# A graph network kernel on one Trainium2 core: two rings of one-hot sets, and the weighted copies dealt anew between GpSimd and ScalarE

## What is computed

```
agg = jax.ops.segment_sum(x[src], tgt, num_segments=n)              # layers 0, 3: plain counts
out = jax.ops.segment_sum(support[src] * edge_weight[:, None], dst)  # layer 1: weighted
agg = jax.ops.segment_sum(concat(nodes[src], edges) @ W_message, dst) # layer 2
```

## Time and profile before

| | |
|---|---|
| median of 3 runs | 1917.61 us (1917.14 to 1918.48) |
| the profiled execution's own time | 1919.31 us |
| its span (first to last instruction) | 1917.4 us |
| PE busy | 1701.7 us (89%), 11659 matmuls |
| DVE busy | 1092.2 us (57%) |
| ACT busy | 759.1 us (40%) |
| POOL busy | 369.2 us (19%) |
| mean granted TensorE clock | 0.952 of 2.4 GHz |
| build stage, first to last L1271 | 46.0 to 577.8 us |

### The profile page before, as it was taken

One profiled execution on the slowest core, in us unless ns is written; L12 is line 12 of the kernel. 1 busy time (PEld: TensorE's weight loads), 2 busy tenths in 40 slices (PEclk: granted clock), 3 DMA queues, 4 the chain that ended last, 5 costly groups with the idle time before them and its releaser, 6 DMA issues.

```text
span 1917.4 us, 47392 instructions
## 1 busy us (share of the span) xinstructions
PE 1701.7 (89%) x11659; PEld 1292.2 (67%) x11660; DVE 1092.2 (57%) x3183; ACT 759.1 (40%) x2194; POOL 369.2 (19%) x982
## 2 busy tenths in 40 slices
PE   2999899999990999999997999999989898986996
PEld 1555555555550777777886888888867676764885
DVE  5888788888888122222333666666536666665111
ACT  0988888989882111111111222222224333331000
POOL 1555555555553000000000000000011111110000
PEclk8999999999995999999998999999999999997998
DMA  2544455445445556553334556565421212110444
GB/s 57 151 147 140 126 155 158 125 125 151 147 146 151 138 171 171 171 171 103 120 132 138 145 153 187 151 179 164 138 90 54 71 54 71 55 68 16 143 150 153
DMA packets 302401, 246.05 MB, mean 128 GB/s; under 512 B 144042, under 2 KB 286182, under 8 KB 302310
## 3 DMA queue, kind: packets, MB, share of 16 engines
q1 hardware_dynamic: 302310, 245.19, 43.0%
HBM read 138.17 MB, written 99.31 MB: 124 GB/s over the span
## 4 chain that ended last, share of the span: by engine, by line
issue 61%; PE 25%; DVE 5%; ACT 2%; POOL 2%; DVEq 1%; ACTq 1%; DMA 1%; SPq 0%; POOLq 0%
PE ps L1271 17%; PE ps L1321 7%; POOL work L601 2%; ACT front L622 2%; DVE front L879 1%; ACT work L616 1%; DVE front L877 1%; DMA wgt_blocks<-arena 0%; DVE work L1000 0%; PE ps L1256 0%; DVE arena L1011 0%; ACTq L350 0%; ACTq L359 0%; ACTq L622 0%; DVE arena L808 0%
## 5 line engine op out<-in xcount | busy, mean ns | idle before, releaser
L1321 PE MATMUL ps<-arena 128*128 128x256 f16 (+1 forms) x5000 | 607.1, 275 | 49.8 <-POOL arena L591 40.2
L1321 PEld LDWEIGHTS ps<-arena 128*128 128x128 f16 x5000 | 489.7, 98 | 147.2 <-issue 77.5
L1271 PE MATMUL ps<-front 128*128 128x400 bf16 x2580 | 482.9, 341 | 23.7 <-ACT front L622 20.0
L622 ACT ACTIVATE front<-front 128x128 bf16<-128x128 bf16 x1290 | 408.9, 391 | 57.6 <-issue 32.6
L1271 PEld LDWEIGHTS ps<-front 128*128 128x128 bf16 x2580 | 241.8, 99 | 196.2 <-ACT front L622 32.0
L1315 PE MATMUL ps<-arena 128*128 128x256 f32 x1250 | 281.3, 382 | 0.0
L579 POOL TENSOR_SCALAR front<-front,w_col 128x128 bf16<-128x128 bf16 x645 | 248.8, 392 | 163.0 <-DVE front L877 156.5
L601 POOL TENSOR_TENSOR work<-work 128x256 f32<-128x256 f32 x75 | 55.2, 736 | 1062.0 <-ACT work L742 1062.0
L1315 PEld LDWEIGHTS ps<-arena 128*128 128x128 f32 x1250 | 237.6, 192 | 31.8
L879 DVE TENSOR_SCALAR front<-iota,off_g,front 128x400 bf16<-128x400 f16 x645 | 253.5, 393 | 0.0
L877 DVE TENSOR_SCALAR front<-iota,front 128x128 bf16<-128x128 f16 x645 | 164.6, 255 | 91.0 <-PE ps L1271 70.0
(11 more groups left out here) (189 smaller groups left out, 1571.8 us busy)
## 6 DMA issues: line engine op xcount, KB each, us to landing
arena<-turned_blocks SPq DMA_DIRECT2D x75, 800.0 KB, 4.3
wgt_blocks<-arena SPq DMA_DIRECT2D x25, 1600.0 KB, 8.5
arena<-wgt_blocks SPq DMA_DIRECT2D x25, 1600.0 KB, 8.3
cnt_blocks<-work SPq DMA_DIRECT2D x25, 800.0 KB, 4.2
turned_blocks<-arena SPq DMA_DIRECT2D x25, 800.0 KB, 3.5
e_raw<-edge_features_padded SPq DMA_DIRECT2D x25, 576.0 KB, 7.9
edge_features_padded<-in_edge_attr SPq DMA_DIRECT2D x24, 512.0 KB, 9.6
out<-arena SPq DMA_DIRECT2D x24, 128.0 KB
```

Source lines behind the costliest of these rows:

```text
L622: m = act.activation(part_of(u, O_SW + a * P, P), part_of(u, O_S, P), ACT.Copy, scale=one(col[:, c, :], t))
L1271: return pe.matmul(out_, left, right, start=False, stop=True, skip_group_check=True)
L1321: m = pe.matmul(agg[par][:, 0:wide], BLK16[par][:, b * P:(b + 1) * P], ZH[zin(i)][:, b * ZW + part * D:b * ZW + part * D + wide], start=(b ...
```

## The change

- A second ring, `ring1`, in the memory of `e_part`, which this stage does not use. Groups of even number in a chunk use the first ring, those of odd number the second (`ring[i % 2]`). Before, one ring of three sets served all.
- DVE keeps for each ring how many sets must be used before it is free (`free_at`), and so may fill one ring while PE still reads the other. It no longer takes the weights from PSUM. Its loop covers single chunks now.
- ACT makes one weighted copy of each set (w0) in place of two, and takes both banks, counts and weights.
- POOL makes the copies for w1 and w2, each for a whole triple in one `tensor_tensor` of 128 x 3 x 128 with the three columns of weights broadcast along the last dimension. It waits for all three S first. Its copy of the columns (L576) and the drains beside it are gone.
- PE's twelve matmuls of a triple are the same; it waits for each weighted copy apart.

```diff
-        ring = front[:, 6 * NCOL:6 * NCOL + RING * SETW // 2].bitcast(BF16)
+        ring0 = front[:, 6 * NCOL:6 * NCOL + RING * SETW // 2].bitcast(BF16)
...
+        ring1 = e_part[:, :, :, :].rearrange("p t a f -> p (t a f)")[:, 0:RING * SETW]
+        ring = [r.rearrange("p (u s) -> p u s", u=RING) for r in (ring0, ring1)]
...
-                def weigh_last(k, u, t, i):
-                    if u == 0:
-                        pool.drain()
-                        chain(pool.tensor_copy(w_col[:, :], col[:, C_W2, bass.ds(t, RING)]))
-                    wait(pool, s_hotS, k + (u + 1))
+                def weigh_sets(k, u, t, i):
+                    if u:
+                        return
+                    wait(pool, s_hotS, k + RING)
                     pool.sem_inc(s_made, 1)
-                    pool.tensor_scalar(part_of(u, O_SW + 2 * P, P), part_of(u, O_S, P), w_col[:, u:u + 1], 1.0,
-                                       ALU.mult, ALU.mult).then_inc(s_hotP, 1)
+                    plain = ring[i % 2][:, :, O_S:O_S + P]
+                    for a, col_of in ((1, C_W1), (2, C_W2)):
+                        into = ring[i % 2][:, :, O_SW + a * P:O_SW + (a + 1) * P]
+                        by = col[:, col_of, bass.ds(t, RING)].rearrange("p (t o) -> p t o", o=1)
+                        pool.tensor_tensor(into, plain, by.broadcast_to([P, RING, P]), ALU.mult
+                                           ).then_inc(s_hotP[a - 1], RING)
...
                 act.activation(stage_c[par][:, t, :], cnt_ps[t % 2][:, 0:GW], ACT.Copy).then_inc(s_taken, 1)
+                act.activation(stage_w[par][:, t, :], wgt_ps[t % 2][:, 0:GW], ACT.Copy).then_inc(s_takenW, 1)
...
-                for a, c in enumerate((C_W0, C_W1)):
-                    m = act.activation(part_of(u, O_SW + a * P, P), part_of(u, O_S, P), ACT.Copy,
-                                       scale=one(col[:, c, :], t))
-                m.then_inc(s_hotA, 1)
+                act.activation(part_of(i, u, O_SW, P), part_of(i, u, O_S, P), ACT.Copy, scale=one(col[:, C_W0, :], t)
+                               ).then_inc(s_hotA, 1)
...
-                dve.tensor_copy(stage_w[par][:, t, :], wgt_ps[t % 2][:, 0:GW]).then_inc(s_takenW, 1)
...
-                    wait(dve, s_used, k + (u + 1))
+                    was = dve.snap(free_at[i % 2], min_val=0, max_val=1 << 20)
+                    wait(dve, s_used, was + (u + 1))
...
+                    if u == RING - 1:
+                        dve.reg_add(free_at[i % 2], step_of[mybir.EngineType.DVE], RING)
...
-                    product(cnt_ps[i % 2][:, 0:GW], part_of(u, O_S, P), part_of(u, O_Q, GW))
-                    wait(pe, s_hotA, k + (u + 1))
-                    for a in range(2):
-                        product(wgt_ps[i % 2][:, 0:GW], part_of(u, O_SW + a * P, P), part_of(u, O_Q, GW))
-                    wait(pe, s_hotP, k + (u + 1))
-                    product(wgt_ps[i % 2][:, 0:GW], part_of(u, O_SW + 2 * P, P), part_of(u, O_Q, GW)
-                            ).then_inc(s_used, 1)
+                    product(cnt_ps[i % 2][:, 0:GW], part_of(i, u, O_S, P), part_of(i, u, O_Q, GW))
+                    for a, s in enumerate((s_hotA, *s_hotP)):
+                        wait(pe, s, k + (u + 1))
+                        m = product(wgt_ps[i % 2][:, 0:GW], part_of(i, u, O_SW + a * P, P), part_of(i, u, O_Q, GW))
+                    m.then_inc(s_used, 1)
```

More of the change, by code:

```diff
@@ L182, in build @@
         s_hotA = sem("first_weighted_s_ready")
-        s_hotP = sem("last_weighted_s_ready")
+        s_hotP = [sem(f"weighted_s_ready{a}") for a in (1, 2)]
         s_eraw = sem("edge_chunk_loaded")
@@ L338, in edge_chunks, with part_of @@
                 e.reg_add(step_of[kind], step_of[kind], 1)
-        def part_of(u, at, width):
-            return ring[:, u * SETW + at:u * SETW + at + width]
+        def part_of(i, u, at, width):
+            return ring[i % 2][:, u, at:at + width]
         step_of = {}
@@ L616, in take @@
                 act.activation(stage_c[par][:, t, :], cnt_ps[t % 2][:, 0:GW], ACT.Copy).then_inc(s_taken, 1)
+                act.activation(stage_w[par][:, t, :], wgt_ps[t % 2][:, 0:GW], ACT.Copy).then_inc(s_takenW, 1)
             def weigh(k, u, t, i):
                 wait(act, s_hotS, k + (u + 1))
[L621 to L624 removed]
+                act.activation(part_of(i, u, O_SW, P), part_of(i, u, O_S, P), ACT.Copy, scale=one(col[:, C_W0, :], t)
+                               ).then_inc(s_hotA, 1)
             def chunk(c, half, par):
                 wait(act, s_store_c[par], half * 16)
+                act.sem_inc(s_made, 1)
+                wait(act, s_store_w[par], half * 16)
                 walk(act, mybir.EngineType.Activation, c, weigh, after=one_tile_late(take, c, par))
@@ L826, in _ @@
             dve.wait_ge(s_prep_pe, PE_TABLES)
-            w16 = ring[:, 0:NCOL]
+            w16 = ring0[:, 0:NCOL]
             chain.v = PREP_ROWS + 4
@@ L867, in _, with hot_sets @@
             start_walk(dve, mybir.EngineType.DVE)
-            def take(c, par, t):
-                wait(dve, s_built, c * PER + (t + 1))
-                dve.tensor_copy(stage_w[par][:, t, :], wgt_ps[t % 2][:, 0:GW]).then_inc(s_takenW, 1)
-            def hot_and_take(c, half, par):
+            free_at = [dve.alloc_register(f"set_free_at{b}") for b in range(2)]
+            for b in range(2):
+                dve.reg_mov(free_at[b], 0)
+            def hot_sets(c):
                 def hot(k, u, t, i):
-                    wait(dve, s_used, k + (u + 1))
+                    was = dve.snap(free_at[i % 2], min_val=0, max_val=1 << 20)
+                    wait(dve, s_used, was + (u + 1))
                     n = c * PER + i
-                    dve.tensor_scalar(part_of(u, O_S, P), iota1[:, 0:P], one(col[:, C_S, :], t), None,
+                    dve.tensor_scalar(part_of(i, u, O_S, P), iota1[:, 0:P], one(col[:, C_S, :], t), None,
                                       ALU.is_equal).then_inc(s_hotS, 1)
-                    dve.tensor_scalar(part_of(u, O_Q, GW), iota1[:, :], one(off_g, n), one(col[:, C_Q, :], t),
+                    dve.tensor_scalar(part_of(i, u, O_Q, GW), iota1[:, :], one(off_g, n), one(col[:, C_Q, :], t),
                                       ALU.add, ALU.is_equal).then_inc(s_hotQ, 1)
[L883 to L889, removed]
+                    if u == RING - 1:
+                        dve.reg_add(free_at[i % 2], step_of[mybir.EngineType.DVE], RING)
+                walk(dve, mybir.EngineType.DVE, c, hot)
+            with dve.Fori(0, NT) as c:
+                hot_sets(c)
             chain = drained(dve)
```

3 lines of the change are left out of this document (1 added, 2 removed).

## The result

The change makes the kernel slower: 1981.7 us (median of 4 runs, 1971.97 to 1984.29) against 1917.4 before, a ratio of 1.033 with a 95% interval of 1.029 to 1.037. The prediction said 2060 us, with 1995 to 2097 for its own case and 1970 to 2180 over most of the rivals. The direction and the mechanism hold; the size is less than half of what was forecast, +64 in place of +142 us.

The account below looks back on a forecast made before the run. PE was taken to bound the build stage, then DVE and POOL in turn: 215 triples x 3.0 = 645, plus 17 and 12, gives 674 against 531.8 us, +142, so 2060 us; own range 1995 to 2097, overall 1970 to 2180.

Parts of the forecast that it names:

- its own case: Whole kernel: POOL's two long products hold DVE off, 3.0 us a triple, +142 us, 2060 us; chance 0.61.
- What bounds the kernel before: Build stage: PE full inside chunks at 2.17 us a triple; 65 us above that at chunk starts, at most 40 at odd ones.
- POOL keeps DVE out while it reads; DVE and POOL are the bound in turn: Build stage after the change: DVE's S and Q wait behind POOL's products, making 3.0 us a triple against PE's 2.17.
- I take 1.0 us: Duration of each POOL product of 384 elements, extrapolated from products of 256 and memsets; ends 0.61 and 1.10 us.
- the two ways through my cycle: One triple, third S to third S: 3.09 us if Q misses the gap between products, 2.91 if it slips in.
- A product holds DVE off for all but its last 0.12 us: POOL's products of 1.0 us: DVE is held for 0.88 us of each, read from a cast behind a 0.73 us product.
- The ends of my range: Own case: from 2.70 us a triple (products 0.97, Q always through) to 3.17 (products 1.10), so 1995 to 2097 us.
- The second triples of a group: 15 triples sharing the first triple's ring wait for PE: 4.1 us in place of 3.0, 17 us in all.
- The chunk starts, +12 us: 7 us for DVE's first S missing the first gap at 24 starts, 5 for ACT's turns back beyond PE's slack.
- the faster rival: DVE gets through between POOL's reads or products are short; PE stays full, 11 + 10 us saved, 1897 us; chance 0.09.
- its whole instruction: Rival: POOL holds DVE off for its full instruction, nothing passes between products, 3.37 us a triple, 2139 us; chance 0.13.
- The clock: Rival: PE's clock falls to the 1.2 GHz level half the time, 3.55 us a triple, 2178 us; chance 0.12.

Follow-up runs that it names:

- the run with the short ACT loop: The kernel before, with ACT looping over single chunks in place of pairs, the staging slot picked by a register: 1881.4 us, ratio to before 0.981.
- the run on one port: The changed kernel with DVE reading its ramps for S and Q from tiles with gaps: 1902.5 us, ratio to before 0.992.
- S and Q in PSUM: The changed kernel with DVE's S and Q comparing against an f32 ramp in PSUM in place of the f16 one in SBUF: 1985.4 us.
- two rings with short loops: The kernel before plus the second ring, old sharing of copies and takes, ACT and DVE looping over single chunks: 1883.3 us, ratio to before 0.982.

## Why the prediction was wrong, point by point

- **What bounds the kernel before**: held. In the run with the short ACT loop the build stage is 37 us shorter: 32 at the odd starts, and 5 inside the chunks, where the median hardly moves (2.17 to 2.16). One reading was wrong beside it. ACT's 95% adds up two groups of instructions that overlap in the trace; from 85 to 530 us ACT was busy for 396 of 445 us, 89%. So its 2.35 us a triple, more than the 2.17 that a triple takes, was too high by the overlap.
- **POOL keeps DVE out while it reads; DVE and POOL are the bound in turn**: held, shown by the run on one port (79 us back) and by S and Q in PSUM (no duration spread). The cycle has the shape that I wrote down, step by step.
- **"I take 1.0 us" for a product**: this is the step that failed, a term of the sum that was too large. It measured 0.83. The fixed part, 0.19 and not 0.10 us, made the slope from 256 to 384 elements too steep (0.97 where 0.93 is right), I rounded up to 1.0, and the repeated column takes off another 0.09 to 0.10. With 0.83 in its place and nothing else changed, the two ways through my cycle give 2.75 and 2.57 us in place of 3.09 and 2.91. Their middle is 2.66, and 215 x 2.66 + 29 - 531.8 = +69 us, where the stage measured +60.
- **"A product holds DVE off for all but its last 0.12 us"**: the first product leaves 0.19 of its 0.83 us open. My 0.12 came from a wrong pair of rows: the cast of the earlier trace rows writes another type, and the five casts of the same line and form as the one in the earlier trace rows that start free take 0.29 us, not 0.26. So that product held for 0.58 of its 0.73. The short copy of the earlier trace rows had shown an open part of 0.20. With the product's length this puts the hold at 0.64 in place of 0.88. The measured cycle is 0.50 + 0.78 + 0.64 + 0.30 + 0.16 + 0.30 = 2.68 us, against 3.0 predicted and 2.67 in the table. Over 200 groups that is 66 of the 82 us that the stage's forecast (674) was too high; 11 more are the chunk starts.
- **The ends of my range**: 2.70 and 3.17 us a triple do not come out of the cycle as written. With products of 0.97 and Q through it gives 2.85, with products of 1.10 it gives 3.11 and 3.29. By that the lower end would have been 2028 us and not 1995.
- **The second triples of a group**: 4.1 forecast; 6.62 - 2.67 = 3.95 measured. Held.
- **The chunk starts, +12 us**: they cost only 0.05 above the inside groups, 1 us in all. I took ACT's standstill as hidden beneath PE's slack. It did not happen at all: the changed ACT code is shorter, is not fetched again, and leaves no gap. The end is the same; the reason was wrong, and the starts themselves became 44 us cheaper in sum, where the faster rival had counted 11 + 10.
- **The rivals**: POOL's hold is not its whole instruction; the open part at its end let one DVE instruction in each time. The rule of the Trainium skill (SBUF — State Buffer, "Who interferes with whom") keeps the shared pair locked for the whole instruction; by it two products back to back would let none in, and here 0.64 of 0.83 us is held, so the measurement decides. The clock stayed up, at 0.99: PE's idle time comes in pieces of about 0.3 us. The faster rival needs DVE to get through, and that is what the run on one port makes true: 1902 us.
- The four runs of the changed kernel spread over 0.6%, and the four before over 0.2%; in a later round 13 runs of the kernel before spread over 0.6% too. What moves them was not looked into.

## What to carry to other kernels

Before work goes to GpSimd, look for DVE instructions that start just behind a GpSimd one and are longer than their median: that difference tells for how much of the GpSimd instruction DVE is shut out. Busy shares show none of it. An extrapolated duration that enters a cycle twice deserves its fixed part measured, not taken from another operation. Compare a held instruction only with free ones of the same line and form. And read the idle time ahead of a loop's first instruction: where an engine stands still for over 2 us at each turn back, a shorter loop body may be worth more than any new buffer.

## What the runs showed of the hardware

- **A loop that is too long is fetched again at each turn back.** ACT's loop over two chunks, with 96 weighted copies in its code, left ACT idle for 2.9 to 3.1 us at each turn from 85 to 530 us, its table loads included, and the instruction queue carried 77 packets, one of them starting in each standstill. With half the copies (the changed kernel) or one chunk a turn, neither is there: 17 and 20 packets. On DVE's loop over two chunks the register instructions for `free_at` (one for each set, and one or two for each triple) brought the same, 3.4 to 3.9 us a turn and 132 packets; with them in a loop over one chunk (two rings with short loops) it was gone, at 19 packets. The length at which it begins was not measured.
- **GpSimd shuts DVE's S, Q and cast out until shortly before its own end.** The hold is 0.17 of 0.37 us for a copy of 128 elements, 0.58 of 0.73 for the f32 product of 256 (a cast was held there), 0.64 of 0.83 for a product of 384 with the repeated column, and 0.73 of 0.92 with the f32 tile: 0.15 to 0.20 us are left open. A second product right behind the first is 0.06 us longer and leaves 0.25 open.
- **Gaps in a source take DVE off the shared port.** 25 rows of 16 at a pitch of 18, written to one run of 400, take 472 ns and not 373, and are not held by POOL any more (longest 479 ns). The rule cited above agrees.
- **GpSimd's products** take 0.19 us and 1.66 ns an element with a repeated column, 0.18 us and 1.91 ns with a tile, the same for bf16 and f32 tiles.
